# Hats in two pieces, positions ahead of the masks, Z products on 64 rows and between the gathers

## What is computed

```python
m = mean(x); v = var(x); xn = (x - m) / sqrt(v + eps)         # group norm ahead of it
om = conv(xn, offset_w) + offset_b                            # 27 channels per position
offset, mask = om[..., :18], sigmoid(om[..., 18:])
pos_y = clip(base_y + inner_y + off_y, 0, 17)                 # per tap; pos_x likewise
value = (hh*hw*v1 + hh*lw*v2 + lh*hw*v3 + lh*lw*v4) * mask    # bilinear sample of xn
out = einsum('nhwc,cf->nhwf', value, w)                       # 9 taps x 64 channels -> 64
```

## Time and profile before

| | us |
|---|---|
| median of 3 runs | 392.46 (391.75 to 392.54) |
| the profiled execution | 390.11 |
| its span in the profile | 388.2 |
| PE busy | 348.3 (90%) |
| DVE busy | 239.2 (62%) |
| ACT busy | 238.4 (61%) |
| POOL busy | 62.3 (16%) |

### The profile page before, as it was taken

The page is one execution under the profiler, slowest core; times in us unless marked ns, Lnnn a source line. Parts: engine busy times, 40 slices in busy tenths (PEclk is TensorE's granted clock), DMA queues, the critical chain, the costliest instruction groups (busy, mean ns, idle before and its releaser), DMA issues.

```text
span 388.2 us, 14584 instructions
## 1 busy us (share of the span) xinstructions
PE 348.3 (90%) x5457; PEld 203.0 (52%) x5509; DVE 239.2 (62%) x1225; ACT 238.4 (61%) x1125; POOL 62.3 (16%) x139
## 2 busy tenths in 40 slices
PE   7999997888999898999989988999899899988886
PEld 2576674554555555455645554555555455543332
DVE  2498763554757675666666666756665766564443
ACT  2586754625865786678567756865786578534443
POOL 3101100432102110212012102111110211110000
PEclk9999999999999999999999999999999999999999
DMA  8000000000000000000000000000000000000000
GB/s 261 4 2 10 10 12 14 15 2 3 3 3 3 5 3 4 3 5 5 2 3 8 2 3 2 8 2 3 6 4 3 3 6 2 5 2 6 2 3 4
DMA packets 4804, 4.29 MB, mean 11 GB/s; under 512 B 3837, under 2 KB 4286, under 8 KB 4734
## 3 DMA queue, kind: packets, MB, share of 16 engines
q1 hardware_dynamic: 4432, 2.84, 2.6%
q10 hardware_dynamic: 302, 0.52, 0.4%
HBM read 2.57 MB, written 0.26 MB: 7 GB/s over the span
## 4 chain that ended last, share of the span: by engine, by line
PE 40%; ACT 24%; DVE 23%; issue 11%; POOL 1%; DMA 1%; ACTq 0%; DVEq 0%
PE bank L727 15%; DVE bank L1232 10%; ACT E L824 9%; DVE H L1242 7%; ACT bank L896 7%; ACT bank L903 7%; PE bank L396 5%; PE bank L463 3%; PE bank L453 2%; PE bank L424 2%; PE bank L550 2%; PE bank L568 1%; PE bank L680 1%; DVE A L1059 1%; PE bank L637 1%
## 5 line engine op out<-in xcount | busy, mean ns | idle before, releaser
L396 PE MATMUL bank<-FB 128*128 128x512 bf16 (+3 forms) x445 | 129.2, 362 | 9.0 <-issue 7.8
L727 PEld LDWEIGHTS bank<-H,VW 64*32 64x32 f32 x3072 | 52.3, 106 | 108.7 <-DVE H L1242 107.2
L727 PE MATMUL bank<-H,VW 64*32 64x4 f32 x3072 | 74.6, 176 | 20.0 <-DVE H L1242 2.8
L896 ACT ACTIVATE bank<-bank 64x8 f32<-64x8 f32 x256 | 37.6, 147 | 75.7 <-PE bank L727 75.3
L1232 DVE TENSOR_TENSOR_SCAN bank<-bank,SU 64x12 f32<-64x12 f32 x256 | 48.5, 190 | 49.7 <-ACT bank L896 47.3
L1242 DVE SCALAR_TENSOR_TENSOR H<-TO,bank 64x4 f32<-64x4 f32 x256 | 40.8, 159 | 45.8 <-ACT bank L903 36.0
L373 POOL TENSOR_SCALAR E<-E,rinv 128x256 f32<-128x256 f32 x62 | 29.8, 481 | 130.7 <-DVE rinv L1042 130.6
L396 PEld LDWEIGHTS bank<-FB 128*128 128x128 bf16 x497 | 39.0, 98 | 21.1 <-issue 1.9
L903 ACT ACTIVATE bank<-bank 64x4 f32<-64x4 f32 x256 | 38.4, 150 | 16.0
L900 ACT ACTIVATE TO<-bank 64x4 f32<-64x4 f32 x256 | 43.7, 171 | 6.2
L1226 DVE SCALAR_TENSOR_TENSOR SU<-H,bank 64x4 f32<-64x4 f32 x256 | 41.3, 161 | 9.0
(11 more groups left out here) (115 smaller groups left out, 344.3 us busy)
## 6 DMA issues: line engine op xcount, KB each, us to landing
AW<-in_attn_w SPq DMA_DIRECT2D x1, 768.5 KB, 8.0
DW<-in_dcn_w SPq DMA_DIRECT2D x1, 576.0 KB, 6.5
X<-in_x_fm SPq DMA_DIRECT2D x1, 256.0 KB, 3.2
X<-in_x_fm ACTq DMA_DIRECT2D x1, 256.0 KB, 5.2
T<-T0T SPq DMA_DIRECT2D x16, 16.0 KB, 1.8
Y<-YT SPq DMA_DIRECT2D x16, 16.0 KB, 1.8
out_dram<-OUT SPq DMA_DIRECT2D x8, 32.0 KB, 1.4
CW<-in_conv_w SPq DMA_DIRECT2D x1, 243.5 KB, 3.7
```

Source lines behind the costliest of these rows:

```text
L396: nc.tensor.matmul(idle[:, 0:n], FB[:, 0:P], FB[:, 0:n], start=True, stop=True)
L727: mm = nc.tensor.matmul(gate_out(m, gate, r, slice(B * s, B * (s + 1))), VW[0:C, gate, r], H[0:C, (STEPS * m + s - 1) % RING, :], start=Fa ...
L896: nc.scalar.activation(GT[:, :, 1:3].rearrange("p b g -> p g b"), b_cell[m % 2][0:C, 0:2 * P].rearrange("p (g s b) -> p g s b", g=2, b=B)[ ...
```

## The change

- SP issues K right behind X2; ACT loads its table first, waits for X2 to land, and then issues X and LW.
- The eps is added in DVE's instruction for `gvar`; the POOL instruction for it is gone, and POOL waits for the memsets (`zeroed`) instead.
- DVE makes the positions without waiting for the masks; the masks on ACT wait for the positions (`pos_done`), behind four Z copies. MK is finished behind the first two `distances`.
- Hats come in chunks: chunk 0 is taps 0 to 2 of the first image, chunk 1 its taps 3 to 8, chunks 2 to 4 the other images. On DVE `distances` of chunk 2 stands ahead of group 4, those of chunks 3 and 4 ahead of groups 5 and 14; `masked(1)` ahead of group 3. On ACT the later hats stand ahead of taps 4 and 6 (`HATS_AT` is 4).
- A Z product takes only the 64 partitions of its image, so DW is half as large. `z(i)`, i = 0 to 3, is now four matmuls of 288 columns, alternating between the two halves of the partitions. z(0) and z(1) stand around the transposes, z(2) behind turns 0 to 2, z(3) behind turns 3 to 5. The banks are reused by the table `z_frees`.
- On PE gathers 0 to 2 stand behind z(2), ahead of turns 3 to 5; from turns 6 to 8 on the order is as before.
- On ACT copies 0 to 3 of Z stand ahead of the masks, 4 to 7 between the hats of chunks 0 and 1, 8 to 11 ahead of AT copy 6 (behind `hats_relu` of chunk 2), 12 to 15 ahead of AT copy 9.

```diff
@@ -40,7 +40,7 @@
 STEPS = TT
 HC = C // 2
 RING = 2 * STEPS
-HATS_AT = 3
+HATS_AT = 4
 BATCH = 3
 TOKENS_AT = (4, 7, 10)
 CHANNELS_AT = (5, 8, 11)
@@ -120,7 +120,7 @@
         X2 = sb("X2", [P, 2, N])
         X = sb("X", [C, B, N])
         CW = sb("CW", [P, CW_END])
-        DW = sb("DW", [P, 2, TAPS * C])
+        DW = sb("DW", [P, TAPS * C])
         AW = sb("AW", [P, AW_END])
         LW = sb("LW", [C + 1, LW_END])
         VEC = sb("VEC", [P, 5, C])
@@ -196,7 +196,8 @@
         banks = [bank(f"bank{i}") for i in range(8)]
 
         b_misc, b_om, b_omt = banks[0], banks[1], banks[2]
-        b_z = banks[3:8] + banks[0:1]
+        b_z = [banks[i] for i in (3, 4, 5, 6, 7, 0, 3, 4, 5, 6, 7, 3, 6, 7, 5, 3)]
+        z_frees = {6: 0, 7: 1, 8: 2, 9: 3, 10: 4, 11: 6, 12: 9, 13: 10, 14: 8, 15: 11}
         b_at = banks[1:3] + banks[0:1]
         b_cv = banks[4:6]
         b_x, b_y, b_k = banks[3], banks[6], banks[7]
@@ -234,7 +235,7 @@
                              "t_rs", "t1_done", "ln3_done", "xt_mm", "xt_done"))
         centred, x1_done = sem("centred"), sem("x1_done")
         s_neg, gated = sem("s_neg"), sem("gated")
-        st_done = sem("st_done")
+        st_done, pos_done = sem("st_done"), sem("pos_done")
         tp_link = sem("tp_link")
         lw_done, ig_mm, o_mm, gates, o_gate, u_done, cell, tanh_c, h_done = (sem(n) for n in (
             "lw_done", "ig_mm", "o_mm", "gates", "o_gate", "u_done", "cell", "tanh_c", "h_done"))
@@ -242,6 +243,7 @@
         block = ctx.enter_context(nc.Block())
 
         GROUPS = [(b, k) for b in range(B) for k in range(TAPS)]
+        CHUNKS = [(0, slice(0, BATCH)), (0, slice(BATCH, TAPS))] + [(b, slice(0, TAPS)) for b in range(1, B)]
         UNITS = [(hg, b) for hg in range(HG) for b in range(B)]
         NU = len(UNITS)
         LAST = NT * STEPS
@@ -301,6 +303,7 @@
         @block.sync
         def _(sp):
             sp.dma_start(X2[:], x_fm2).then_inc(ld_x, 16)
+            sp.dma_start(K[:], consts).then_inc(ld_k, 16)
             sp.dma_start(CW[:], conv_w).then_inc(ld_cw, 16)
             sp.dma_start(DW[:], dcn_w).then_inc(ld_dw, 16)
             sp.dma_start(AW[:], attn_w).then_inc(ld_aw, 16)
@@ -334,8 +337,8 @@
             nc.gpsimd.memset(SU[:], 1.0).then_inc(zeroed, 1)
             nc.gpsimd.memset(AY[:], 0.0).then_inc(zeroed, 1)
 
+            pool.wait_ge(zeroed, 7)
             pool.wait_ge(gn_var, 1)
-            link(nc.gpsimd.tensor_scalar(gvar[:], gvar[:], GN_EPS, None, ALU.add))
             nc.gpsimd.tensor_tensor(grs[:, :, 0], gvar[:, :, 0], half_neg[:, 0:2], ALU.pow).then_inc(gn_rs, 1)
 
 
@@ -417,12 +420,13 @@
             mm.then_inc(om_mm, 1)
 
             def z(i):
-                b, pt = divmod(i, 2)
-                if i >= 3:
-                    pe.wait_ge(z_sb, 2 * (i - 2))
-                for m in range(2):
-                    nc.tensor.matmul(b_z[2 * (i % 3) + m][:, 0:ZC],
-                                     XC[:, b // 2, P * pt:P * (pt + 1)], DW[:, b % 2, ZC * m:ZC * (m + 1)],
+
+                for n in range(4 * i, 4 * i + 4):
+                    pair, pt, m, h = n // 8, n // 4 % 2, n // 2 % 2, n % 2
+                    if n in z_frees:
+                        pe.wait_ge(z_sb, z_frees[n] + 1)
+                    r = slice(C * h, C * (h + 1))
+                    nc.tensor.matmul(b_z[n][:, 0:ZC], XC[r, pair, P * pt:P * (pt + 1)], DW[r, ZC * m:ZC * (m + 1)],
                                      start=True, stop=True).then_inc(z_mm, 1)
 
             pe.wait_ge(ld_dw, 16)
@@ -435,16 +439,14 @@
                 mm = nc.tensor.transpose(b_omt[:, OFFS2 * i:OFFS2 * (i + 1)], OM[:, j, P * h:P * (h + 1)],
                                          ident[0:OFFS2, 0:OFFS2])
             mm.then_inc(omt_done, 1)
-            for i in range(1, 2 * B):
-                z(i)
-
+            z(1)
 
             def turn(g):
                 pe.wait_ge(a_done, g + 1)
                 if g == 0:
                     pe.wait_ge(dist, 1)
                 if g == 2:
-                    pe.wait_ge(z_sb, 4 * B)
+                    pe.wait_ge(z_sb, 6)
                 elif g >= TURNS:
                     pe.wait_ge(at_sb, g - TURNS + 1)
                 for pt in range(2):
@@ -457,6 +459,8 @@
             def gather(g):
                 b, k = GROUPS[g]
                 pe.wait_ge(at_sb, g + 1)
+                if k == 0 and b < 2:
+                    pe.wait_ge(z_sb, (8, 16)[b])
                 if k == 0 and b >= 2:
                     pe.wait_ge(t0f_done, 2 * (b - 1))
                 for pt in range(2):
@@ -582,7 +586,13 @@
                     values(VALUES_AT.index(j))
                 if j == len(GROUPS) // BATCH:
                     scores(0, 0)
-                if j >= 1:
+                if j == 0:
+                    z(2)
+                    for g in range(BATCH):
+                        gather(g)
+                if j == 1:
+                    z(3)
+                if j >= 2:
                     for g in range(BATCH * (j - 1), BATCH * j):
                         gather(g)
                 if j - 1 in KEYS_AT:
@@ -748,10 +758,10 @@
 
         @block.scalar
         def _(act):
-            act.dma_start(K[:], consts).then_inc(ld_k, 16)
+            nc.scalar.preload_act_table(ACT.Sigmoid)
+            act.wait_ge(ld_x, 16)
             act.dma_start(X[:], x_fm).then_inc(ld_x1, 16)
             act.dma_start(LW[:], lstm_w).then_inc(ld_lw, 16)
-            nc.scalar.preload_act_table(ACT.Sigmoid)
 
 
             act.wait_ge(gn_rs, 1)
@@ -760,41 +770,43 @@
                 nc.scalar.copy(XC[:, j, :].rearrange("p (y x) -> p y x", y=SIDE), XN[:, j, 1:SIDE + 1, 1:SIDE + 1]
                                ).then_inc(xc_done, 1)
 
-            def z_out(i):
-                b, pt = divmod(i, 2)
-                for m in range(2):
-                    act.wait_ge(z_mm, 2 * i + m + 1)
-                    nc.scalar.copy(Z[:, pt, b, :, :].rearrange("p k f -> p (k f)")[:, ZC * m:ZC * (m + 1)],
-                                   b_z[2 * (i % 3) + m][:, 0:ZC]).then_inc(z_sb, 1)
+            def z_out(n):
+                pair, pt, m, h = n // 8, n // 4 % 2, n // 2 % 2, n % 2
+                act.wait_ge(z_mm, n + 1)
+                nc.scalar.copy(Z[:, pt, 2 * pair + h, :, :].rearrange("p k f -> p (k f)")[:, ZC * m:ZC * (m + 1)],
+                               b_z[n][:, 0:ZC]).then_inc(z_sb, 1)
 
             act.wait_ge(om_mm, 1)
             for j in range(2):
                 nc.scalar.activation(OM[:, j, :], b_om[0:OFFS2, N * j:N * (j + 1)], ACT.Identity, bias=OB
                                      ).then_inc(om_low, 1)
-            z_out(0)
-
-            act.wait_ge(omt_done, 1)
+            for n in range(4):
+                z_out(n)
+
+            act.wait_ge(pos_done, 1)
             for i in range(4):
                 j, h = divmod(i, 2)
                 src = b_omt[:, OFFS2 * i:OFFS2 * (i + 1)].rearrange("p (b o) -> p b o", b=2)[:, :, 18:27]
                 nc.scalar.activation(MK[:, 2 * j:2 * j + 2, :, h], src, ACT.Tanh, scale=0.5).then_inc(mask_act, 1)
 
-            def hats_abs(b):
-                v = HAT[:, :, b, :, :, :].rearrange("p d k h v -> p d (k h v)")
-                act.wait_ge(dist, b + 1)
+            def hats_abs(c):
+                b, k = CHUNKS[c]
+                v = HAT[:, :, b, k, :, :].rearrange("p d k h v -> p d (k h v)")
+                act.wait_ge(dist, c + 1)
                 nc.scalar.activation(v, v, ACT.Abs).then_inc(hat_abs, 1)
 
-            def hats_relu(b):
-                v = HAT[:, :, b, :, :, :].rearrange("p d k h v -> p d (k h v)")
-                act.wait_ge(hat_abs, b + 1)
+            def hats_relu(c):
+                b, k = CHUNKS[c]
+                v = HAT[:, :, b, k, :, :].rearrange("p d k h v -> p d (k h v)")
+                act.wait_ge(hat_abs, c + 1)
                 nc.scalar.activation(v, v, ACT.Relu, bias=1.0, scale=-1.0).then_inc(hat_act, 1)
 
-            z_out(1)
-            z_out(2)
             hats_abs(0)
             hats_relu(0)
-            for i in range(3, 2 * B):
-                z_out(i)
+            for n in range(4, 8):
+                z_out(n)
+            hats_abs(1)
+            hats_relu(1)
             def tokens_out(b):
                 act.wait_ge(t0_mm, b + 1)
                 act.wait_ge(ln0_st, b + 1)
@@ -834,9 +846,12 @@
 
             for g, (b, k) in enumerate(GROUPS):
                 if k == HATS_AT and b + 1 < B:
-                    hats_abs(b + 1)
+                    hats_abs(b + 2)
                 if k == HATS_AT + 2 and b + 1 < B:
-                    hats_relu(b + 1)
+                    hats_relu(b + 2)
+                if g in (6, 9):
+                    for n in range(8, 12) if g == 6 else range(12, 16):
+                        z_out(n)
                 act.wait_ge(at_mm, g + 1)
                 if g >= SLOTS:
                     act.wait_ge(cv_mm, g - SLOTS + 1)
@@ -938,7 +953,8 @@
             dve.wait_ge(gn_avg, 1)
```

(53 more changed lines are left out.)

## The result

The changed kernel takes 395.91 us (median of 6 runs, 394.11 to 396.87), the kernel before, run beside it, 391.54 (389.96 to 392.54): a ratio of 1.0105 with a 95% interval of 1.0072 to 1.0137. It is 4.4 us slower, where +2.4 had been forecast. The profiled execution took 394.11 us with a span of 392.3, against 390.11 and 388.2: +4.1 in span. The profiled execution is the fastest of the six; the other five have spans of 393.3 to 395.0 us and a lower mean clock (0.991 and 0.987 against 0.995).

What follows compares the result with a forecast made beforehand. Z on PE was taken as a true cost ahead of the recurrent steps. Head -0.69, z(3) +2.24 and hats +0.86 gave +2.4 us on the 392.46 median: 394.86, stated as 394.8 us, range 392.9 to 397.3.

Steps and rivals of the forecast that it cites:

- rival 1: PE's clock falls in idle gaps ahead of turn 0 or z(3), slowing products behind: 396.8 to 399.2 us; chance 0.12.
- the three parts: Head -0.69, wait at z(3) +2.24, hats of images 2 and 3 +0.86 us; low ends +1.0, high ends +4.0.
- Head: Kernel start: POOL's eps instruction gone (0.32 us) and X2 landing sooner without K (0.37): -0.69 us, bounds -0.3 to -0.8.
- First hats, z(2), gathers: Front part: first A 1.9 us earlier, at 17.41 before the head's gain; z(2) 1.2 us; gathers 0 to 2 at 21.24.
- z(3): PE waits behind turns 3 to 5 for ACT's copies 8 to 11, delaying turn 6: +2.24 us, bounds +1.8 to +3.2.
- Hats of images 2 and 3: Later relu on ACT delays DVE's `masked` and YT by 0.43 us per image: +0.86 us, bounds 0 to +1.1.
- Sum of the waits: Whole kernel: -0.69 + 2.24 + 0.86 = +2.4 us over the kernel before.
- What bounds the kernel: Front part ahead of the recurrent steps: PE busy without a gap from 13 to 32 us, Z a true cost on PE.
- The drain: Tiling mode changes drain PE: about 0.1 us in the rows; two more switches around z(2) and z(3) cost 0.2 to 0.4.

Runs made afterwards that it cites:

- hats back: Changed kernel with the hats of images 2 and 3 on ACT ahead of taps 3 and 5 again, those of image 1 left: 395.08 us, ratio 1.0107.
- dummies in the first gap: Changed kernel with 22 dummy matmuls on PE between z(1) and turn 0 only, the wait ahead of z(3) left idle: 394.13 us, ratio 1.0064.
- dummies in both: Changed kernel with dummy matmuls in both PE gaps, ahead of turn 0 and ahead of z(3): 392.59 us, ratio 1.0044.
- the copies moved alone: Changed kernel with Z copies 8 to 11 ahead of AT copy 3 instead of AT copy 6 on ACT: 391.12 us against 390.64, ratio 1.0.
- both moves: Changed kernel with Z copies 8 to 11 ahead of AT copy 3 and hats of images 2 and 3 ahead of taps 3 and 5: 391.62 us, ratio 1.0008.
- dummies ahead of z(3): Changed kernel with 22 dummy matmuls of 224 columns on PE in its wait ahead of z(3): 392.80 us, ratio 1.0069.
- Filling a gap: Changed kernel with copies 8 to 11 and later hats moved earlier, plus 22 dummy matmuls between z(1) and turn 0: 389.05 us against 391.13, ratio 0.9929.

## Why the prediction held, and where it was off

The direction, the waits and the range held; the size was 2 us short, +4.4 where +2.4 was forecast, since rival 1, the clock, came on top of the waits. Rival 1 had a chance of 0.12, and its low end, 396.8, is +4.3 over the 392.46 that it was counted from: as a difference that is what was measured. Luck had a part in the range and in the level. The high ends of the three parts gave only +4.0, so it was the piece of rival 1 inside the range that covered the result; and 395.91 lies only 1.1 us from the forecast's 394.8 because the kernel before took 391.54 this time and not 392.46.

- **Head.** Forecast -0.69, measured -0.55 (XN at 7.21 instead of 7.76). X2's statistics start 0.48 sooner, more than my 0.37, and POOL's instruction gave about what was asked. What I missed is PE: its clock rose only behind the averaging in this execution, so that matmul took 0.56 instead of 0.36 us and DVE got its result 0.2 later. Where it took 0.36 (the traces of hats back, of dummies in the first gap and of dummies in both), the offset convolution starts at 7.74 to 7.89 instead of 8.64, a gain of 0.75 us and more.
- **First hats, z(2), gathers.** First A forecast at 16.7, measured 17.01 (the head's 0.14 and masks and POS that each came a little later); z(2) 1.2 us, measured 1.17; copy 8 of Z forecast at 25.43 (26.12 - 0.69), measured 25.45.
- **z(3).** With the clock kept up turn 6 starts at 27.58; forecast was 27.54 (25.99 + 2.24 - 0.69). This step was right almost to the row, with some luck: my own working ended at 28.4, which gives 27.7, and the sum took less; and a first A that came 0.3 late was made up for by a chain on ACT that was shorter than I had added up (AT 3 to copy 8 2.60 us instead of 2.72).
- **Hats of images 2 and 3.** Forecast +0.43 twice. Measured 0.38 (3.68 - 3.30) and 0.25, and 0.6 in the spans of the two kernels that differ only in the hats (the copies moved alone, and both moves). The second is smaller: ACT started relu 0.16 us behind the start of the token copy (49.42 and 49.58), where it was 0.32 the first time (37.80 and 38.12). I had carried the first image's numbers over.
- **Sum of the waits.** +2.4 forecast, +2.5 measured in the spans with both gaps filled. The front of the traces gives a little less: the head -0.55, z(3) +2.14 (27.58 - 25.99 + 0.55) and the hats +0.63 are +2.2. The recurrent steps differ by some tenths between executions (from the first scan on DVE to the issue of the last output 293.95 us in the kernel before, 294.34 in the one with dummies ahead of z(3)), so that 2.4 and 2.5 agree to 0.1 is partly chance.
- **The clock.** This is the step that failed. I made the fall a rival of its own with a chance of 0.12, and in all six runs of the changed kernel it seems to be there: spans 392.3 to 395.0 at a mean clock of 0.995 down to 0.987, where the kernel with both gaps filled has 390.5 to 390.8 at 0.998 to 1.0. "No clock fell in the 388 us" was true of one execution of the kernel before, and I took it as evidence for gaps that were twice as long as any in it. A fall belonged into the sum with its price and not beside it: one fall behind z(3) costs 1.6 us on the path (I had said about 2), or 2.8 where it lasts longer, and one behind the first gap 1.3 us (I had said 4.4). The profiled execution has one fall; the other five, with spans 1.0 to 2.7 us longer, have more or longer ones. By the Trainium skill, "TensorE: Matmul & The Clock Gate", section HAM oscillation, idle time between bursts throttles the engine; the trace agrees, 0.52 granted from 28 to 30 us behind 2.5 us of idle time, though the waits in that section's example are longer than this one. I had cited it and not let it raise the chance.
- **What bounds the kernel.** I wrote that Z is a true cost on PE since A was ready 1.7 us before PE. The kernel before with Z on 64 rows says no: ACT's 16 copies end at the same moment, so cutting PE's part alone is worth nothing (lowest spans 388.1 to 388.3 against 388.2 to 388.9). My forecast did not rest on that sentence, but a forecast for such a change would have failed by it.
- **The drain.** Leaving the 64-row shape was priced at 0.17 us in z(2)'s 1.2; z(2)'s measured 1.17 us agrees (2 x 0.48 + 0.2) and doesn't show more.

What stays open: why the clock falls in one execution of a kernel and not in another behind the same gap, and what makes the spans of 389.5 us and more of the kernel before. Six of them, 389.5 to 389.8, have a mean clock of 0.999 or 1.0, so no fall explains those; the landing of the last output may. The others have 0.991 to 0.998, which for most suggests falls. Its one profiled execution shows none; two traces of its relatives show a fall at 71 to 72 us in the attention stage, and one a clock that rose late at the start, with the offset conv at 9.59 instead of 8.64 us.

## What to carry to other kernels

When work is moved between two engines' queues, write down for each moved product the instruction that empties the bank it needs, and what stands ahead of that on the other engine: here four copies stood behind five other instructions while ACT had just idled for 2.6 us. Price a new PE wait of the size seen here (2.5 us) together with the half clock that may follow it (1.3 to 2.8 us here), and fill such gaps with dummy matmuls into a bank that nobody reads. When two engines end a stage together, halving the work of one shows nothing.

## What the hardware did that I had not expected

- PE's clock fell behind 2.4 to 2.5 us of idle time in an otherwise dense stretch (0.50 granted at 18 to 20 us with the hats back, 0.52 at 28 to 30 us in the changed kernel), in most executions but not all, and it fell also in the attention stage behind idle pieces of 0.3 to 1.3 us.
- Filling a gap made the kernel not only faster but steady: 388.73 to 389.08 us over 11 runs, where the same kernel without dummies spread from 389.51 to 392.53.
- The rise at the start varies too. The second set of eight dummies took 1.89 us in the kernel before, 2.13 in the changed one and 3.57 in the one with Z on 64 rows, and there the work behind it waited.
- The last 32 KB of output took 1.4 us to land in one execution and 3.2 in another, enough to move a span from one cluster to the next without any change of the clock.
